# Cosine-gated convolution with two-expert feed-forward: neighbours fetched by SBUF to SBUF transfers, and start, steps and end reordered

## What is computed

```python
# first branch: a = cosine similarity of ctx at t with ctx at t-1, t, t+1
sim = stack([cos(e, e_left), cos(e, e), cos(e, e_right)])       # (B, 3, T), over the 128 channels
att = repeat(sim, C, axis=1)                                    # row i of the unfolded input gets sim[i // C]
inp = unfold(layernorm(x), K=3)                                 # (B, 3*C, T), row c*K + k is channel c at t+k-1
x = x + tanh(g_xattn) * einsum('bit,oi->bot', inp * att, w)
# second branch: 8 experts of rank 16, the top two for every row of 1024
f = layernorm(x)
gates = top2(softmax(f @ router_w.T + router_b)), normalised to sum 1
x = x + tanh(g_ffn) * sum_e gates_e * (f @ A_e.T) @ Bm_e * 0.5
```

## Time and profile before

| | us |
|---|---|
| median of three runs | 221.23 |
| the profiled execution, its own time | 221.01 |
| its span | 219.2 |
| TensorE busy | 207.7 |
| VectorE busy | 165.5 |
| ScalarE busy | 115.0 |
| GpSimd busy | 113.9 |

### The profile page before, as it was taken

How to read it: one execution, slowest core, us unless ns; L and a number is a source line. 1 busy time by engine, 2 the same in 40 slices (tenths; PEclk the granted TensorE clock), 3 DMA queues, 4 the chain that set the end, 5 groups by cost and what they waited for, 6 DMA issues and landing times.

```text
span 219.2 us, 4498 instructions
## 1 busy us (share of the span) xinstructions
PE 207.7 (95%) x1470; PEld 128.9 (59%) x1470; DVE 165.5 (75%) x423; ACT 115.0 (52%) x211; POOL 113.9 (52%) x233
## 2 busy tenths in 40 slices
PE   7899999997999999999999999999999999999963
PEld 7765776465474656566565756464755565646641
DVE  1465585874989889797979697978788687777573
ACT  4672849857836465475555665645437453321220
POOL 3464662696585857564767566585450515131310
PEclk9999999999999999999999999999999999999999
DMA  5798951050251707143333423222305020202204
GB/s 180 231 334 257 379 176 53 0 196 1 96 187 42 250 19 241 34 149 142 149 141 125 150 111 99 97 96 86 108 0 191 4 96 0 100 0 96 97 0 191
DMA packets 14644, 26.89 MB, mean 123 GB/s; under 512 B 1694, under 2 KB 10142, under 8 KB 14622
## 3 DMA queue, kind: packets, MB, share of 16 engines
q1 hardware_dynamic: 14622, 26.61, 34.4%
HBM read 18.22 MB, written 8.39 MB: 121 GB/s over the span
## 4 chain that ended last, share of the span: by engine, by line
PE 77%; POOL 7%; DVE 6%; issue 4%; ACT 2%; DMA 1%; SPq 0%; POOLq 0%; ACTq 0%; DVEq 0%
PE conv_ps L940 33%; PE hidden_ps L964 12%; PE xT_ps L950 6%; PE out_ps L981 4%; PE hidden_ps L871 4%; PE sim_ps L929 4%; POOL rinv L370 3%; PE out_ps L985 3%; PE out_ps L982 3%; PE out_ps L997 2%; PE out_ps L972 2%; DMA et<-ctx 1%; PE xT_ps L915 1%; PE xT_ps L884 1%; DVE qp L607 1%
## 5 line engine op out<-in xcount | busy, mean ns | idle before, releaser
L940 PE MATMUL conv_ps<-pt,wT 128*128 128x512 f32 x192 | 98.8, 598 | 0.0
L679 DVE TENSOR_TENSOR pt<-xn,sim_ps 128x512 f32<-128x512 f32 x96 | 60.0, 680 | 5.4 <-PE sim_ps L929 4.6
L506 ACT ACTIVATE xT<-xT_ps 128x512 f32<-128x512 f32 x32 | 19.1, 597 | 56.4 <-PE xT_ps L950 56.4
L964 PEld LDWEIGHTS hidden_ps<-aT,xT 128*128 128x128 f32 x256 | 33.1, 190 | 8.4 <-issue 7.9
L964 PE MATMUL hidden_ps<-aT,xT 128*128 128x136 f32 x256 | 35.1, 280 | 0.0
L370 POOL TENSOR_TENSOR rinv<-nmax,minus_half 128x8 f32<-128x8 f32 x16 | 26.7, 1669 | 14.9 <-DVE nmax L616 14.9
L940 PEld LDWEIGHTS conv_ps<-pt,wT 128*128 128x128 f32 x192 | 31.8, 193 | 4.4 <-issue 1.5
L950 PEld LDWEIGHTS xT_ps<-wide,x 128*128 128x128 f32 x128 | 15.6, 141 | 16.7 <-issue 15.4
L361 POOL TENSOR_TENSOR qp<-qp 128x1024 f32<-128x1024 f32 x8 | 19.0, 2380 | 11.2 <-DVE qp L607 11.2
L686 DVE TENSOR_TENSOR x<-conv_ps,xt 128x512 f32<-128x512 f32 x32 | 21.8, 682 | 1.3 <-PE conv_ps L940 1.3
L691 DVE BATCH_NORM_STATS2 bn<-x 128x6 f32<-128x512 f32 x32 | 21.9, 683 | 0.0
(11 more groups left out here) (106 smaller groups left out, 293.1 us busy)
## 6 DMA issues: line engine op xcount, KB each, us to landing
xt<-x SPq DMA_DIRECT2D x16, 512.0 KB, 3.3
out<-x SPq DMA_DIRECT2D x15, 512.0 KB, 2.6
et<-ctx SPq DMA_DIRECT2D x14, 514.0 KB, 4.5
aT_in<-expert_aT SPq DMA_DIRECT2D x1, 544.0 KB, 7.7
et<-ctx SPq DMA_DIRECT2D x2, 257.0 KB, 2.9
bm_in<-expert_b SPq DMA_DIRECT2D x1, 512.0 KB, 8.8
out<-x SPq DMA_DIRECT2D x2, 256.0 KB, 2.0
et<-ctx SPq DMA_DIRECT2D x1, 385.5 KB
```

What stands on the lines that cost most here:

```text
L506: nc.scalar.activation(xT[:, n % 2, 4 * h:4 * h + 4, :].rearrange("p c n -> p (c n)"), xT_ps[:, :], ACT.Copy).then_inc(xT_out, 1)
L679: nc.vector.tensor_tensor(pt[:, i, :], xn[:, n % 2, h * HALF + t:(h + 1) * HALF + t], sim_ps[:, t, :], ALU.mult).then_inc(mod_done, 1)
L940: nc.tensor.matmul(conv_ps[h][:, :], wT[:, t * P:(t + 1) * P], pt[:, i, :], start=(t == 0), stop=(t == TAPS - 1)).then_inc(tap_done, 1)
L964: last = nc.tensor.matmul(h_ps, xT[:, n % 2, c, :], aT[:, c, :], start=(c == 0), stop=(c == KC - 1))
```

## The change

For the third and all later groups `next_norms` is gone. In its place SyncE issues four SBUF to SBUF transfers (`move_norms`) into a new tile `moved`, as soon as `dr` is there, and `similarities` reads that tile and waits for `moved_done`. For these groups the split of the similarities, the transposes and the copies of the rows now lie one step later (steps 3, 6, 9, 12), and in their middle.

Beside it the change reorders and edits:
- **Start.** The identity comes between the two halves of the first context load, and square and product of the first sample go by halves. The product of sample 2 moves from GpSimd to VectorE, context 2 is loaded earlier, `sum_context` runs one or two samples sooner, `expert_means` is split in two and fills the place of ten `keep_warm` calls, and the centring of `aT` comes after the first three `modulate` of sample 1.
- **Weights.** `hidden_out` scales by `rs2` and waits for it and for the logits; the logits wait for TensorE's `h_done` alone. Both weights are made on ScalarE as two sigmoids (`expert_weights`, behind `feature_squares` on its queue as before), and two small GpSimd operations are gone.
- **Steps.** `experts_out(n-2, 0)` comes behind the step's first `tap`.
- **End.** `experts_out(13, 1)` moves out of step 15 behind it. The last sample's output is made, added and stored in four quarters, into four PSUM banks; the weights' operations come ahead of `finish(14, 0)`.

```diff
@@ SyncE
+            def move_norms(q):
+                if q >= 3:
+                    sp.wait_ge(sim_done, 3 * q)
+                first, last, r = slice(0, (KC - 1) * G), slice(G, KC * G), rinv[:, q % 2, :]
+                sp.wait_ge(partial, 2 * q + 1)
+                sp.dma_start(moved[0:P - 1, 0, :], r[1:P, :]).then_inc(moved_done, 16)
+                sp.dma_start(moved[P - 1:P, 0, first], r[0:1, last]).then_inc(moved_done, 16)
+                sp.dma_start(moved[1:P, 1, :], dr[0:P - 1, :]).then_inc(moved_done, 16)
+                sp.dma_start(moved[0:1, 1, last], dr[P - 1:P, first]).then_inc(moved_done, 16)
...
                 if n + 7 < B:
                     load_e(n + 7)
+                if n in CHAINED:
+                    move_norms(CHAINED[n])
@@ ScalarE
             def hidden_out(n):
+                i = n % 2
                 act.wait_ge(h_done, n + 1)
+                act.wait_ge(logit_done, n + 1)
+                act.wait_ge(rs2_done, n + 1)
...
-                nc.scalar.activation(hs[:, n % 2, :], h_ps[:, 0:ER], ACT.Copy).then_inc(h_out, 1)
+                nc.scalar.activation(hs[:, i, :], h_ps[:, 0:ER], ACT.Copy, scale=rs2[:, i:i + 1]).then_inc(h_out, 1)
@@ VectorE, similarities
-                dve.wait_ge(rnext_done, q + 1)
+                if q < 2:
+                    dve.wait_ge(rnext_done, q + 1)
+                else:
+                    dve.wait_ge(moved_done, 64 * (q - 1))
+                r_next, d_last = (rnext_ps, dlast_ps) if q < 2 else (moved[:, 0, :], moved[:, 1, :])
@@ VectorE, step n
                     for k in range(TAPS, STEPS):
+                        take(chain)
                         modulate(STEPS * n + k)
+                    if n - 1 in CHAINED:
+                        take(chain)
+                        rows_low(CHAINED[n - 1])
                     finish(n - 2, 0)
                     token_stats(n - 1, 1)
                 if n in CHAINED:
                     take(partials(CHAINED[n]), 2)
+                    chain = similarities(CHAINED[n])
                 if n > 2:
                     token_variance(n - 1)
-                take(chain, 2)
-                for _ in range(3):
-                    take(picks)
-                    take(chain)
+                take(picks, 3)
                 residual(n, 0)
-                take(chain)
...
                 token_stats(n, 0)
+                take(chain, 2)
                 if n in SQUARED:
                     product(SQUARED[n])
-                if n in CHAINED:
-                    rows_low(CHAINED[n])
@@ TensorE, step n
-                experts_out(n - 2, 0)
                 tap(STEPS * n)
+                experts_out(n - 2, 0)
...
                 tap(STEPS * n + 1)
+                if n - 1 in CHAINED:
+                    transpose_similarities(CHAINED[n - 1], tokens + 1, turned)
+                    passed += 1
                 experts_in(n - 1, 1)
-                if n in CHAINED:
-                    next_norms(CHAINED[n], tokens + 1)
                 tap(STEPS * n + 2)
@@ TensorE, end
+            experts_out(B - 3, 1)
+            experts_in(B - 1, 1)
             experts_out(B - 2, 0)
-            experts_in(B - 1, 1)
             experts_out(B - 2, 1)
             transpose_hidden(B - 1)
-            experts_out(B - 1, 0)
-            experts_out(B - 1, 1)
+            for w in range(4):
+                experts_out_last(w)
```

241 lines of the change are left out of this document (132 added, 109 removed).

## The result

The changed kernel takes **228.08 us** (median of four runs, 227.16 to 228.92) where the kernel before took 221.10 beside it: ratio 1.029, interval 1.023 to 1.035. It is slower by 7 us; the forecast was 218.3, range 214.0 to 221.0. The profiled execution took 228.92 us (span 227.1), so against the profiled execution of before (span 219.2) 7.9 us have to be found.

The account below looks back on a forecast made before the run. It took TensorE's own time to bound the steps and chains of engines the start and end: 221.0 - 3.3 - 2.4 + 0 + 4.2 - 1.2 = 218.3 us, range 214.0 to 221.0.

Parts of the forecast that it names:

- transposes owed to the next step: 24 transposes that stood before step 2's last tap come one step later: 0.6 us of the gain there only owed.
- Term 4: The four transfers, from dr to similarities: they land in time, 0; by the dearest row up to 1 us four times.
- rival C: Transfers come late, VectorE waits at similarities: each us beyond 8 from dr costs 1 us, four times; chance 0.05.
- Term 5: Steps 3, 6, 9, 12: a new wait from the later split, 1.05 us a step, plus 4.2 us in all.
- Rival A: Steps 3, 6, 9, 12: no new wait, time 214.1, or 216.2 if half goes; chance 0.28 whole or half.
- Terms 1 and 2: Start to the end of step 2: reordered chain comes earlier, minus 3.3 us in all, bounds minus 1.5 to minus 6.
- term 1: Start up to the second group's rows: spread at 26.2 instead of 29.95, minus 3.7 us, bounds minus 2 and minus 4.
- term 2: Second group's rows to the end of step 2: last tap from 58.81 to about 54.9, minus 3.9 including term 1.
- Rival B: Start gives back its gain, as step 2's chains keep their order: only minus 0.9 there, time 220.7; chance 0.12.
- Rival D: TensorE's clock falls because idle matmuls are gone; no price could be read, given nothing and no chance.
- Term 3: Steps 5, 8 and 11: next_norms gone from TensorE, 0.81 us three times, minus 2.4 us.
- Term 6: The end: experts_out(13,1) moved out of step 15, last output by quarters, minus 1.2 us, bounds minus 0.5 and minus 1.9.

Follow-up runs that it names:

- the early turn: Changed kernel with transfers before the context load, product(1) later, whole split in the chain's step, similarities transposed behind the next step's tap 0 and experts_out: 219.80 us, ratio 0.988.

## Why the prediction was wrong

By its own terms, in the profiled executions (219.2 and 227.1 us of span):

| term | forecast | measured | how |
|---|---|---|---|
| 1 and 2, to the end of step 2 | -3.9 | -1.6 | start of step 3 |
| transposes owed to the next step | +0.6 | +0.6 | 24 transposes once more, 0.56 |
| 3, `next_norms` gone | -2.4 | -2.7 | 4.45 less three times 0.6 |
| 4, transfers | 0 | **+4.8** | step 9, 18.58, less the 13.82 with the transfers ahead |
| 5, the new wait | +4.2 | **+7.1** | 2.54 + 2.50 + 2.42 (13.82 - 11.40) + 2.06 less four times 0.6 |
| 6, the end | -1.2 | -0.3 | steps 13, 14 and from 15 to the end |
| sum | -2.7 | +7.9 | |

- **Term 4 is the step that failed.** "On SyncE the load of x and of context stand ahead and are issued by then" was read from step 5 and taken for all four. Context 15, loaded in step 8, comes in three pieces, and the trace of before had its row with an issue of 3.81 us; the forecast did not use that row, and it delayed nothing there. The mechanism was rival C's (VectorE at `moved`, `product` and `hidden_rest` behind it), but in one step and by the issue, not by the landing: in step 8 VectorE goes on 2.3 us after the last issue begins (132.17 to 134.51), and in steps 2, 5 and 11 it waits for no transfer. C's price (1 us each, four times) and its 0.05 were both wrong. The runs with the transfers ahead and with 112 and 15 partitions show the cause from two sides. The rule of the Trainium skill ("DMA: Bandwidth & Descriptors", Why a DMA increments its semaphore by 16 and not by 1) on how transfers are dealt out speaks against 127 partitions, and the forecast weighed the fixed cost of a transfer instead. The section of the Trainium skill that it cites for that cost ("DMA: Bandwidth & Descriptors", Anatomy of one DMA) describes transfers issued by GpSimd, while these are issued by SyncE; the 2.3 us above are close to it. Two of the four transfers have 127 partitions themselves, and with no such load ahead the one behind them takes 0.79 to 0.88 us of issue. Why the first transfer behind the load is issued in 0.7 us and the second stalls stays open; the long issues in the change (2.69 and 5.34 us) and with two pieces (20.75 and 4.45) are all those of one-partition transfers.
- **Term 5 was the right mechanism, mis-sized.** Of the 2.9 us too little, 1.9 are the split beside the `fold`, which the list of durations took at 0.24 as if VectorE were alone; moving one cast gave them back. The rest is smaller: TensorE waits in step 6 0.45 for `x` and 0.47 for `hw` (0.6 and 0.45 forecast), in step 12 0.45 and 1.02. These rows count a little less than the delay: in step 6 the tokens' transposes start 1.47 us after the tap ahead of them (103.68, 105.15), where 0.86 stood before, so they come 0.61 late. Rival A, no new wait, is refuted in the change; the early turn came near it in step 12 alone.
- **Terms 1 and 2 were right as a layout and wrong in their durations.** The start of the change, unedited, stood in six profiles. In four of them `product(1)` came behind the power's start and start 3 at 55.74, 56.00, 56.24 and 56.45 (the last with the matmuls back in step 2): -3.3 to -4.0, where -3.9 was said. Even so two errors cancel in that number: sample 1's rows were spread at 26.95 to 27.45 there and not at 26.2, so term 1 was 0.8 to 1.2 us too large and what term 2 adds to it too small by about as much. In the other two `product(1)` met the power (2.65 us) and start 3 came at 57.37 and 58.15, the latter with the clock at 0.50 behind it. The layout took the power at its 1.67. The halved first load, of which 0.5 us were hoped, gave nothing: with the identity between, the second half was ready at 5.0 to 5.9 in these profiles, and before the whole at 4.41. Rival B (the start gives back its gain) had the effect, not the mechanism. Rival D, the clock, was given nothing of its own; it fell behind TensorE's wait of 3.42 us in step 9 and behind that of 1.33 in the start, but not behind that of 1.46 at 43.63 in the same execution. That idle matmuls are gone, D's reason, was not tested by a run of its own.
- **Term 3** holds, twice: 0.9 a step by the change's table, and 0.9 when the matmuls were put back.
- **Term 6** missed by 0.9, and by more in the end itself: from the start of step 15 to the end nothing changed (-0.06). Two parts of it cancel.

```profile
220.70 0.33 PE L1019 MATMUL out_ps<-wide,hw 128*128 128x128 f32 x1 [0.86 <-DVE hw L787]
...
222.66 2.26 SPq L346 DMA_DIRECT2D out<-x  x4
```

The last transpose of `hw` comes 14.99 us after the start of step 15 where it came 15.86 after it (213.61 in the earlier trace rows): 0.9 gained, where 1.2 was forecast. From there to the end it takes 6.4 us, where it took 5.6: 0.8 lost, in the part that was to gain by the quarters. The first store is issued 1.3 us earlier against step 15, but the four take 2.26 us of issue where the two took 1.02, so the last of them starts only about 0.1 us earlier. Two halves took 6.1.

## What to carry to other kernels

Before putting transfers on a queue, read how long every issue takes that stands ahead of them in every step, not in one typical step: a long issue that delays nothing today is the price of the next thing behind it. Cut transfers so that the partition count divides well; one piece of 127 partitions cost more than two of 112 and 15. When a small VectorE operation that lies on a chain is moved, look at what GpSimd runs at the new place, for its duration is not its own there; and where two starts are within 0.1 us of each other, expect either order.
